# Collecting on a graph layer: six split tiles per bucket in place of four, five one-hots made by GpSimd, and first halves of rows loaded two buckets ahead

## The reference

```python
msgs = edge_vals[:, None] * x[edge_col]
agg = jax.ops.segment_sum(msgs, edge_row, num_segments=n)
h = (1.0 + eps[0]) * x + agg
h = _bn_relu(h @ W1 + b1, g1, be1)
h = _bn_relu(h @ W2 + b2, g2, be2)
```

## Time and profile before

| | |
|---|---|
| median of 3 runs | 3237.8 us (3237.02 to 3244.94) |
| the profiled execution | 3250.25 us, its span 3248.4 us |
| granted TensorE clock, mean | 0.956 of full speed |
| PE / DVE / ACT / POOL busy | 88% / 74% / 50% / 25% of the span |
| DMA moved | 710.52 MB, mean 219 GB/s |

### The profile page before, as it was taken

How to read it: one execution, slowest core, us unless ns; L and a number is a source line. 1 busy time by engine, 2 the same in 40 slices (tenths; PEclk the granted TensorE clock), 3 DMA queues, 4 the chain that set the end, 5 groups by cost and what they waited for, 6 DMA issues and landing times. The chain is left out here.

```text
span 3248.4 us, 70401 instructions
## 1 busy us (share of the span) xinstructions
PE 2860.7 (88%) x20204; PEld 2392.9 (74%) x20205; DVE 2408.5 (74%) x5908; ACT 1618.7 (50%) x3203; POOL 823.2 (25%) x885
## 2 busy tenths in 40 slices
PE   4887678888888887999999999987999999599998
PEld 2333477777777776888888888755777777499998
DVE  8998967677777765888888888766666666666665
ACT  3664456566666663222222222575777777533332
POOL 4221045555555552000000000021222222122222
PEclk9888889999999998999999999998999999799999
DMA  2332077778777777999999999100344444566664
GB/s 56 106 115 74 20 261 291 279 283 306 290 292 283 284 288 298 330 335 333 345 332 327 333 329 332 49 0 26 131 157 178 155 174 159 215 211 211 214 214 135
DMA packets 214806, 710.52 MB, mean 219 GB/s; under 512 B 28495, under 2 KB 104313, under 8 KB 189514
## 3 DMA queue, kind: packets, MB, share of 16 engines
q1 hardware_dynamic: 130778, 405.55, 36.7%
q0 software_dynamic: 83952, 304.02, 24.1%
HBM read 383.91 MB, written 340.05 MB: 223 GB/s over the span
## 5 line engine op out<-in xcount | busy, mean ns | idle before, releaser
L1437 PE MATMUL coll_ps_sum<-coll_rows,coll_hot 128*128 128x256 f32 x2940 | 657.4, 380 | 23.5 <-DVE coll_hot L1372 23.2
L1088 PE MATMUL send_ps_msg<-send_parts,send_pick 128*128 128x256 f32 x3584 | 558.6, 300 | 108.1 <-ACT send_msg L1128 86.6
L1437 PEld LDWEIGHTS coll_ps_sum<-coll_rows,coll_hot 128*128 128x128 f32 x2940 | 550.1, 190 | 101.5 <-DVE coll_hot L1372 28.3
L1088 PEld LDWEIGHTS send_ps_msg<-send_parts,send_pick 128*128 128x128 f32 x3584 | 476.3, 198 | 129.8 <-DVE send_pick L991 78.3
L943 POOL DMA_INDIRECT messages<-send_msg,send_to x448 | 468.9, 1047 | 379.9 <-ACT send_msg L1128 235.9
L1128 ACT ACTIVATE send_msg<-send_ps_msg 128x1024 f32<-128x1024 f32 x448 | 454.1, 1027 | 221.7 <-PE send_ps_msg L1088 158.3
L991 DVE TENSOR_SCALAR send_pick<-send_ps_local,edges_down 128x512 fp32r<-128x512 f32 x448 | 334.2, 746 | 209.5 <-PE send_ps_local L1076 136.4
L1372 DVE TENSOR_SCALAR coll_hot<-coll_nodes,coll_rows 128x128 f32<-128x128 f32 x1470 | 393.4, 340 | 2.2 <-DMA coll_rows<-messages 0.8
L1491 ACT ACTIVATE nodes_hid<-coll_ps_turned 128x256 f32 (+1 forms) x98 | 37.5, 383 | 553.1 <-PE coll_ps_turned L1269 553.1
L1566 POOL CAST lin_x_hi<-lin_hT 128x1024 fp32r<-128x1024 f32 x25 | 29.2, 1168 | 940.1 <-ACT lin_hT L1702 887.4
L2033 DVE TENSOR_TENSOR gate_act_lo<-gate_act_h,gate_act_hi 128x512 fp32r<-128x512 f32 x200 | 141.7, 709 | 167.5 <-ACT gate_act_hi L1942 126.3
(11 more groups left out here) (335 smaller groups left out, 5887.2 us busy)
## 6 DMA issues: line engine op xcount, KB each, us to landing
coll_rows<-messages SPq DMA_DIRECT2D x98, 1300.0 KB, 7.3
coll_rows<-messages SPq DMA_DIRECT2D x98, 1170.0 KB, 7.3
exp_pay<-regions SPq DMA_DIRECT2D x105, 646.0 KB
send_window<-node_rows SPq DMA_DIRECT2D x112, 128.0 KB
node_rows<-sort_xn SPq DMA_DIRECT2D x25, 512.0 KB, 5.0
coll_own<-node_rows SPq DMA_DIRECT2D x98, 128.0 KB, 4.1
sort_xt<-in_x_dram SPq DMA_DIRECT2D x24, 512.0 KB, 4.3
layers_w<-in_x_dram SPq DMA_DIRECT2D x24, 384.0 KB
```

The lines of the kernel that those rows point to most:

```text
L1088: ins = pe.matmul(ps_msg[:, q % 2, a, :], pick[:, q * RUN + a, :], parts[:, s % 2, part, :], start=(part == 0), stop=(part == 1))
L1437: ins = pe.matmul(ps_sum[:, s, 0:D], hot_of(s, j), features(u, j), start=(j == CX), stop=(j == CJ - 1))
```

## The change

`CX` goes from 4 to 6: tiles 4 and 5 become split tiles, on every engine. `CL = 14`: the one-hots of tiles 14 to 18 are made by GpSimd, from a copy of the node numbers of its own (`marks`), and TensorE waits for them (`last_ready`) ahead of tile 14. SyncE issues the first half of bucket b + 2 in bucket b, ahead of the second half of b, with a table load of its own.

```diff
@@ -59,7 +59,8 @@
 CROWS = CAPR * RUN
 CJ = CROWS // P
 CA = 10
-CX = 4
+CX = 6
+CL = 14
 NO_SOURCE = 127 * P
 FAR = float(1 << 20)
 SCALE = 2048.0
@@ -1185,6 +1186,7 @@
 
         hot = m.sb("hot", [P, 2 * (CA - CX) + CJ - CA, P])
         nodes = m.sb("nodes", [P, P])
+        marks = m.sb("marks", [P, P])
         own = m.sb("own", [P, 2, D])
         sums = m.sb("sums", [P, 2, D])
         src_col = m.sb("src_col", [P, GT], I32)
@@ -1199,6 +1201,8 @@
         rows_in = [[m.sem(f"rows_in{r}{h}") for h in range(2)] for r in range(CH)]
         own_in = [m.sem(f"own_in{s}") for s in range(2)]
         hot_ready = m.sem("hot_ready")
+        marks_ready = m.sem("marks_ready")
+        last_ready = m.sem("last_ready")
         high_ready = m.sem("high_ready")
         rest_ready = m.sem("rest_ready")
         added = m.sem("added")
@@ -1278,19 +1282,28 @@
             def _(sp):
                 general = sp.value_load(c.flag[0:1, 0:1], min_val=0, max_val=1)
 
+                def part(b, u, h):
+
+                    j0, j1 = HALVES[h]
+                    at = sp.value_load(c.starts[0:1, ds(b, 1)], min_val=0, max_val=MAXRUNS * RUN)
+                    mine = messages[ds(at, CROWS), :].rearrange("(p j) f -> p j f", p=P)
+                    if h == 0 and later(b, CH):
+                        sp.wait_ge(added, 2 * (b - CH) + 1)
+                    if h == 1 and later(b, 2):
+                        sp.wait_ge(added, 2 * (b - 2) + 2)
+                    sp.dma_start(rows[:, u] if h == 0 else rows2[:, u % 2], mine[:, j0:j1, :]).then_inc(rows_in[u][h], 16)
+
                 def bucket(b, u, i):
                     s = u % 2
-                    at = sp.value_load(c.starts[0:1, ds(b, 1)], min_val=0, max_val=MAXRUNS * RUN)
-                    mine = messages[ds(at, CROWS), :].rearrange("(p j) f -> p j f", p=P)
-                    for h, (j0, j1) in enumerate(HALVES):
-                        if h == 0 and later(b, CH):
-                            sp.wait_ge(added, 2 * (b - CH) + 1)
-                        if h == 1 and later(b, 2):
-                            sp.wait_ge(added, 2 * (b - 2) + 2)
-                        sp.dma_start(rows[:, u] if h == 0 else rows2[:, s], mine[:, j0:j1, :]).then_inc(rows_in[u][h], 16)
+                    if later(b, 1) and (not isinstance(b, int) or b + 2 < NBK):
+                        part(b + 2, (u + 2) % CH, 0)
+                    part(b, u, 1)
                     if later(b, 2):
                         sp.wait_ge(sums_ready, b - 1)
                     sp.dma_start(own[:, s, :], plain[ds(b * P, P), :]).then_inc(own_in[s], 16)
+                    if isinstance(b, int) and b == 0:
+                        part(1, 1, 0)
+                        part(2, 2, 0)
 
                 def slow_bucket(b, u, i):
 
@@ -1308,6 +1321,7 @@
                 with sp.If(general):
                     buckets_in_turn(sp, slow_bucket)
                 with sp.Else():
+                    part(0, 0, 0)
                     all_buckets(sp, bucket)
                 layers.load(sp)
 
@@ -1332,8 +1346,28 @@
 
                     chunks_in_turn(pool, chunk)
 
+                def bucket(b, u, i):
+                    s = u % 2
+                    if later(b, 1):
+                        pool.wait_ge(last_ready, b)
+                        pool.sem_inc(pool_turn, 1)
+                    pool.tensor_scalar(marks[:], marks[:], float(P), None, ALU.add).then_inc(marks_ready, 1)
+                    pool.wait_ge(marks_ready, b + 2)
+                    pool.wait_ge(rows_in[u][1], 16 * (i + 1))
+                    if later(b, 1):
+                        pool.wait_ge(added, 2 * (b - 1) + 2)
+                    pool.sem_inc(pool_turn, 1)
+                    for j in range(CL, CJ):
+                        ins = pool.tensor_scalar(hot_of(s, j), marks[:], node_of(u, j), weight_of(u, j), ALU.is_equal, ALU.mult)
+                    ins.then_inc(last_ready, 1)
+
                 with pool.If(general):
                     buckets_in_turn(pool, slow_bucket)
+                with pool.Else():
+                    pool.tensor_scalar(marks[:], c.line[:], float(-P), None, ALU.add).then_inc(marks_ready, 1)
+                    pool.wait_ge(marks_ready, 1)
+                    pool.sem_inc(pool_turn, 1)
+                    all_buckets(pool, bucket)
 
             @block.vector
             def _(dve):
@@ -1368,7 +1402,7 @@
                             wide = [P, CX, P]
                             dve.tensor_tensor(exact[:, s], nodes[:].unsqueeze(1).to_broadcast(wide),
                                               rows[:, u, 0:CX, ROW_ID].unsqueeze(2).to_broadcast(wide), ALU.is_equal)
-                        for j in range(max(j0, CX), j1):
+                        for j in range(max(j0, CX), min(j1, CL)):
                             ins = dve.tensor_scalar(hot_of(s, j), nodes[:], node_of(u, j),
                                                     weight_of(u, j), ALU.is_equal, ALU.mult)
                         ins.then_inc(hot_ready, 1)
@@ -1434,6 +1468,9 @@
                         if h == 0 and later(b, 2):
                             pe.wait_ge(sums_ready, b - 1)
                         for j in range(max(j0, CX), j1):
+                            if j == CL:
+                                pe.wait_ge(last_ready, b + 1)
+                                pe.sem_inc(pe_turn, 1)
                             ins = pe.matmul(ps_sum[:, s, 0:D], hot_of(s, j), features(u, j),
                                             start=(j == CX), stop=(j == CJ - 1))
                         if h == 0:
```

## The result

The changed kernel is slower: 3262.26 us median (3257.54 to 3266.62, 8 runs) against 3242.87 (3237.02 to 3255.37, 8 runs), a ratio of 1.0058 with a 95% interval of 1.0044 to 1.0072. The forecast was 3221, in a range from 3196 to 3255: the measured time lies above the range, and the change went the other way. The profiled execution took 3265.95 us with a span of 3264.1, 15.7 longer than that of before.

The account below looks back on a forecast made before the run. It took TensorE's 7.64 us plus 0.33 of lateness as the present pace, 7.97 a bucket; afterwards the loop's 7.59 + 0.2 = 7.79. So -0.18 x 97 = -18, + 1 at the start: 3237.8 - 17 = 3221 us, range 3196 to 3255.

Parts of the forecast that it names:

- TensorE's saving: On TensorE, two more split tiles lower its own work by 0.39 us a bucket, to 7.25.
- The early loads: First halves asked for some three buckets ahead remove the cause of 0.33 us a bucket, 32 us in the stage.
- The loop: Once-a-bucket path through TensorE, ScalarE and VectorE, turn to turn: 7.26 us before, 7.59 after, then setting the pace.
- GpSimd's five one-hots: GpSimd makes five one-hots at 0.3 to 0.5 us each, in time for TensorE up to 1.0 us each.
- The contention: GpSimd's one-hots meet VectorE's remainders in the loop, raising 7.59 by 0.2 us a bucket.
- Rival 4: GpSimd's one-hots come late for TensorE, from 1.07 us each; at 1.5 us each, 3445 us; chance 0.06.
- rival 2: TensorE sets the pace after all, at 7.25 to 7.45 us a bucket, 3169 to 3188 us; chance 0.05.
- rival 3: GpSimd's operations hold VectorE up in the loop, 8.1 to 9.0 us a bucket, 3250 to 3340 us; chance 0.12.
- rival 5: Second halves become the late loads, 7.9 us a bucket or more, no difference; within that outcome's chance of 0.15.

Follow-up runs that it names:

- g1: Changed kernel with ScalarE's `keep` one bucket later and three GpSimd one-hots in place of five; 7.36 us a bucket, 0.9834 of the kernel before.
- e1: Kernel before with the early loads alone, four split tiles and all one-hots by VectorE; 7.71 us a bucket, 0.9944 of the kernel before.
- g3: Changed kernel with four split tiles and three GpSimd one-hots, early loads kept; 7.62 us a bucket, 0.992 of the kernel before.
- e2: Kernel before with six split tiles alone, loads and one-hots as before; 8.85 us a bucket, 1.0274 of the kernel before.
- e4: Changed kernel with four GpSimd one-hots in place of five, VectorE making tile 14's; 7.89 us a bucket, 0.9975 of the kernel before.
- f1: Changed kernel with ScalarE's `keep` of bucket b - 2 behind `high` of b; 7.96 us a bucket, 1.0004 of the kernel before.
- e3: Kernel before with five one-hots by GpSimd alone, four split tiles and late loads; 7.65 us a bucket, 0.9913 of the kernel before.
- f2: Changed kernel with two sets of buffers for GpSimd's one-hots, so it may start a bucket earlier; 7.98 us a bucket, 1.0015 of the kernel before.
- f3: Changed kernel with both the later `keep` and two buffer sets for GpSimd's one-hots; 7.82 us a bucket, 0.9953 of the kernel before.
- f4_price: Kernel before with 18 more GpSimd operations whose results nobody reads, to price them; 3100.12 us in its one run.

## Why the prediction was wrong

**TensorE's saving** was right: 0.39 us a bucket, as the shortest intervals show (7.63 before, 7.25 in g1).

**The early loads** were right, and e1 shows their gain alone: 18.8 us where 0.33 us a bucket would have been 32. The rest of that lay in the loop, 0.4 us under TensorE's work, where small unevenness still comes through: g3, which has the short loop beside the early loads, comes to 7.62 where e1 has 7.71.

**The loop** as a path was right, and its length nearly: e2 went to 8.85 (8.89 without the last interval) where 8.87 was reckoned, and e4 to 7.89 where 7.85 was. That 7.85 is the 7.59 of the prediction with 0.26 more for VectorE's one-hots, which the prediction did not have.

**The step that failed is "GpSimd's five one-hots".** It took 0.3 to 0.5 us each, from a copy's price per element, and concluded "in time, up to 1.0 us each". A one-hot costs 0.79 with nothing in its way. Arithmetic on GpSimd is not priced like a copy: 0.52 for one operation of this size where the copy takes 0.29. The bound was too wide as well: of the 5.1 us between the half before and TensorE's need the signals take 0.59, which leaves 0.90 a one-hot and not 1.0.

**The contention was put on the wrong engine.** The meeting itself was foreseen, from a row in which VectorE had to wait for GpSimd. That row is no exception: the 20 operations of its VectorE line that began under a copy, 0.57 to 0.79 us into it, took 0.79 to 1.01 us, and each ended 0.54 or 0.55 after the copy. The forecast adds 0.2 us for it on VectorE, in the loop; that is my estimate, and no run shows it. In its place the runs showed remainders that lost nothing (480 ns, 478 before), and four one-hots on VectorE, for which the forecast charged nothing, that took 1.30 where 1.03 was reckoned. That alone would have left the forecast standing, since 7.72 is under its 7.79. It was GpSimd that lost, about 0.5 us at the first and at the fourth one-hot, 1.34 and 1.31 for 0.79, which makes 5.33 out of 3.95 for the series with smaller losses at the others. The gating row shows VectorE second and late; the changed kernel's trace shows the other direction, GpSimd second and late, beside `exact` (0.76 us after its end) and beside the remainders (0.67 or 0.79 after the last). The prediction priced only the first.

**Rival 4 is what happened**, with a chance of 0.06. Its break-even was 1.07 us per one-hot; 5.33/5 is 1.07 as well, and yet the pace was 8.12 and not 7.97: most of that is the signals, 0.59 in sum and not 0.4. Four one-hots in place of five (e4) ended TensorE's wait for GpSimd, and taking the loop away (f1) did not. Neither cause alone would have done it: at 0.79 each the cycle is 6.7 us and the loop's 7.6 would have decided, close to the forecast; that is reckoned and not run on this kernel, but e3 shows series of 4.1 us that TensorE does not wait for.

**The other rivals.** No interval came at TensorE's floor (rival 2), and no remainder was stretched (rival 3, whose time is near the measured one, but by another mechanism). Second halves (rival 5) were late for GpSimd 16 times in 91, 38.6 us, so they had a small part; f2 and f3 show that they stand right behind GpSimd's start as the next limit.

## What to carry to other kernels

When work moves to an idle engine, price it by a row of the same operation or by a measured one, not by a cheaper operation per element, and write down its cycle (when it may start, how long it takes, who waits) as carefully as that of the busy engines. Where operations of two engines hold each other up, as a one-hot under `exact` did here (1.31 us for 0.79), ask for each engine what it loses, and weigh the one that has the least slack. Look for a loop through several engines that lies just under the bound, as here 7.26 us under 7.64: shortening it (e3) brought more than removing the lateness (e1), and both together brought no more than the first alone (g3).

## What the runs showed of the hardware

- VectorE's one-hots were slowed beside GpSimd after all, though not always: the four of the second half took 1.37 us in the timeline above, while the four of the first half at 1609.56, beside GpSimd too, took 1.11, which is what four took before (3 x 0.257 + 0.34); 1.37 and 1.11 are also the medians over all buckets. The mean of all went from 340 to 380 ns. The prediction charged nothing for them. Why some lose and others do not stays open.
- Between GpSimd's one-hot and `exact` it counted which began first, and in e3 a lead of 0.12 us was enough. With 0.12 to 0.2 us of lead GpSimd kept its 0.79 in all 14 cases of e3, and `exact` took 0.78 to 0.87 for 0.69. With less it came out either way: at 0.116 ahead GpSimd took 1.31 in e3 and 1.57 in the changed kernel, at 0.07 to 0.09 ahead it kept 0.79 three times. The remainders can lose a little too: in e4 73 of the 588 took 0.51 and one 0.59 beside GpSimd, where the median is 0.48.
- GpSimd took 0.38, 0.42 and 0.53 us for 4 elements a partition with two scalars from memory (f4_price), and 0.195 as a median for 4 with immediates.
- DMA moved 358 GB/s over 677 us at a share of 0.96 (g1), where it moved 333 over 758 us at 0.91 before.
